# Cross parts of a recurrence in FP32 instead of split fp32r, and a layer norm written once per tile

## The reference

```python
# layer 0: Fourier mixing, then an MLP
xn = layernorm(x) ; xf = rfft2(xn)                    # per image and channel
o1 = relu(einsum(xf, w1c) + b1c)                      # blocks of 24 channels, real and imaginary apart
xs = irfft2(o1)
x  = xs + x + gelu(layernorm(xs) @ w1 + b1) @ w2 + b2 # 192 -> 768 -> 192
# layer 1: gated recurrence, then an MLP
xn = layernorm(x)
u = xn @ Wu + bu ; g = sigmoid(xn @ Wg + bg)
h = 0
for _ in range(8): h = g * (h @ A) + (1 - g) * u      # A is 192 x 192
x = x + h
x = x + gelu_tanh(layernorm(x) @ w1 + b1) @ w2 + b2
```

## Time and profile before

| | us |
|---|---|
| median of 3 runs (lowest, highest) | 1198.21 (1192.73, 1200.53) |
| the profiled execution, its own time | 1196.19 |
| span of the profile, first to last instruction | 1194.4 |
| PE matmul, PE weight load, DVE, ACT, POOL busy | 1079.7, 875.7, 853.9, 696.7, 363.5 |
| mean granted clock of the PE | 0.956 |

### The profile page before, as it was taken

The page is one execution under the profiler, slowest core; times in us unless marked ns, Lnnn a source line. Parts: engine busy times, 40 slices in busy tenths (PEclk is TensorE's granted clock), DMA queues, the critical chain, the costliest instruction groups (busy, mean ns, idle before and its releaser), DMA issues. The chain is left out here.

```text
span 1194.4 us, 26159 instructions
## 1 busy us (share of the span) xinstructions
PE 1079.7 (90%) x9256; PEld 875.7 (73%) x9256; DVE 853.9 (71%) x2230; ACT 696.7 (58%) x1293; POOL 363.5 (30%) x383
## 2 busy tenths in 40 slices
PE   3659999985797999999799999999999699999998
PEld 1358888873486888888567767767677488888887
DVE  6645556442899988777768689689698767676665
ACT  3736556542664567666677567567545266766665
POOL 1250111211699200000238438338247311021110
PEclk9879999896898999999899999999999799999999
DMA  7888799896100000000100000000000000000001
GB/s 179 272 183 169 149 168 185 154 208 163 49 1 1 0 0 0 0 0 0 47 1 2 1 1 1 1 1 1 1 1 1 0 14 27 26 27 26 26 26 40
DMA packets 140186, 64.19 MB, mean 54 GB/s; under 512 B 115808, under 2 KB 134912, under 8 KB 140096
## 3 DMA queue, kind: packets, MB, share of 16 engines
q1 hardware_dynamic: 132888, 37.42, 15.5%
q0 software_dynamic: 5568, 18.73, 5.8%
q10 hardware_dynamic: 1648, 6.91, 1.8%
HBM read 44.17 MB, written 12.58 MB: 48 GB/s over the span
## 5 line engine op out<-in xcount | busy, mean ns | idle before, releaser
L904 ACT ACTIVATE L_conv_hf<-L_conv_ps,L_conv_b 128x512 f32<-128x512 f32 x192 | 132.1, 688 | 184.4 <-PE L_conv_ps L1075 175.7
L1094 PE MATMUL L_conv_ps<-w2hl,L_conv_hhi 128*128 128x384 f32 x768 | 229.2, 366 | 4.1 <-DVE X L990 4.1
L980 DVE TENSOR_TENSOR L_conv_hlo<-L_conv_hf,L_conv_hhi 128x512 fp32r<-128x512 f32 x192 | 140.9, 750 | 78.5 <-ACT L_conv_hhi L913 76.4
L1094 PE MATMUL L_conv_ps<-w2hl,L_conv_hlo 128*128 128x192 f32 x768 | 188.6, 252 | 0.0
L1209 POOL TENSOR_TENSOR sc_lo<-XS,sc_hi 128x512 fp32r<-128x512 f32 x96 | 142.9, 1504 | 116.1 <-ACT sc_hi L1285 116.1
L1487 PE MATMUL sc_ps<-sc_hi,wh 128*128 128x512 f32 (+1 forms) x440 | 160.8, 437 | 3.4 <-ACT XS L1269 3.2
L1094 PEld LDWEIGHTS L_conv_ps<-w2hl,L_conv_hhi 128*128 128x128 f32 x768 | 144.4, 188 | 8.7 <-DVE L_conv_hlo L980 3.4
L1487 PE MATMUL sc_ps<-sc_hi,wl 128*128 128x512 f32 (+1 forms) x440 | 147.8, 392 | 0.0
L1094 PEld LDWEIGHTS L_conv_ps<-w2hl,L_conv_hlo 128*128 128x128 f32 x768 | 146.2, 191 | 0.0
L636 PE MATMUL psF<-spectrum,X 100*24 100x64 f32 x4352 | 128.9, 290 | 15.2 <-issue 11.2
L861 POOL TENSOR_TENSOR X<-X,L_conv_b 128x192 f32 x128 | 83.2, 681 | 194.4 <-DVE L_conv_xn L964 194.4
(11 more groups left out here) (135 smaller groups left out, 2028.0 us busy)
## 6 DMA issues: line engine op xcount, KB each, us to landing
X<-in_L_conv_w SPq DMA_DIRECT2D x136, 144.0 KB
XS<-in_x POOLq DMA_DIRECT2D x8, 768.0 KB, 6.9
rows_spectrum<-XS POOLq DMA_DIRECT2D x8, 768.0 KB, 4.2
d<-rows_spectrum ACTq DMA_DIRECT2D x8, 768.0 KB, 5.5
X<-in_x SPq DMA_DIRECT2D x8, 768.0 KB, 8.2
out<-X SPq DMA_DIRECT2D x15, 384.0 KB, 2.6
XS<-d POOLq DMA_DIRECT2D x59, 96.0 KB, 4.7
spectrum<-in_L_conv_mlp_w SPq DMA_DIRECT2D x2, 576.0 KB, 9.3
```

The source lines that it names most:

```text
L904: nc.scalar.activation(hf[:, m % 3, :], ps[:, RB + m % 2, :], gelu, bias=b1[:, m:m + 1]).then_inc(act1, 1)
L980: nc.vector.tensor_tensor(hlo[:, m, :], hf[:, m % 3, :], hhi[:, m, :].bitcast(F32), ALU.subtract).then_inc(h_lo, 1)
L1094: mm = pe.matmul(o, x, w, start=(m == 0 and n == 0), stop=(m == MT - 1 and n == 1), skip_group_check=True)
```

## The change

In the scan, the cross parts A01 and A10 of the state products of steps 2 to 7 (those whose state is positive and whole in one buffer) are made by one FP32 matmul each from the unsplit state, in a new function `state_product`; step 1 and the projections keep `product`. The two A01 matmuls have 64 output columns and write partitions 0 to 63 and 64 to 127 of one bank; the two A10 matmuls have 64 rows and write two banks. They stand between the high and the low parts. `mm` is counted per tile, at the three low matmuls that end the product, and ACT and POOL wait for the count of their own tile. Three more DMAs load A01 once and A10 into both halves of the partitions.

In the MLP the DVE writes each normalised tile once (192 channels), the transposes of the last channels have 64 stationary columns and alternate with the full ones, ACT writes the 64 rows of the last channels twice into `y`, and the POOL waits for the normalised tiles in the first MLP as well.

```diff
+        self.a01, self.a10 = sb("a01", [P, C1]), sb("a10", [P, P])
...
+        loads += [(self.a10[C1 * k:C1 * (k + 1), :], t["L1_conv_A"][P:C, 0:P]) for k in range(2)]
...
-        xn = sb("xn", [P, GT, 2 * P])
+        xn = sb("xn", [P, GT, C])
...
             def group(i):
-                if XS is None:
-
-                    pool.wait_ge(normed, GT * (i + 1))
+                pool.wait_ge(normed, GT * (i + 1))
...
-                    nc.scalar.activation(y[:, k, :], ps[:, TB + k, :], ACT.Identity, bias=bet[:, k:k + 1],
-                                         scale=gam[:, k:k + 1]).then_inc(y_done, 1)
+                    rows = P if k == 0 else C1
+                    for to in range(0, P, rows):
+                        ins = nc.scalar.activation(y[to:to + rows, k, :], ps[0:rows, TB + k, :], ACT.Identity,
+                                                   bias=bet[0:rows, k:k + 1], scale=gam[0:rows, k:k + 1])
+                    ins.then_inc(y_done, 1)
...
-                    for to, fr in ((slice(0, C), slice(0, C)), (slice(C, 2 * P), slice(P, C))):
-                        ins = nc.vector.tensor_scalar(xn[:, k, to], SRC[:, n, fr], mv[:, n, 0:1],
-                                                      rs[:, bass.ds(n, 1)], ALU.subtract, ALU.mult)
-                    ins.then_inc(normed, 1)
+                    nc.vector.tensor_scalar(xn[:, k, :], SRC[:, n, :], mv[:, n, 0:1], rs[:, bass.ds(n, 1)],
+                                            ALU.subtract, ALU.mult).then_inc(normed, 1)
...
-                for k in range(2):
-
-                    passed(pe, y_done, 2 * (i - 1) + k + 1)
-                    for j in range(GT):
...
+                passed(pe, y_done, 2 * i)
+                for j in range(GT):
+                    pe.wait_ge(normed, GT * i + j + 1)
+                    for k, (rows, cut) in enumerate(((P, slice(0, P)), (C1, slice(P, C)))):
+                        mm = pe.transpose(ps[0:rows, TB + k, P * j:P * j + P], xn[:, j, cut], ident[:, :])
+                        if j == GT - 1:
+                            mm.then_inc(tposed, 1)
...
-                    pool.wait_ge(q["mm"], MM * i + 3 * (s + 2))
+                    pool.wait_ge(q["mm"], MM * i + 3 * (s + 1) + (3 if s == 1 else place[j]))
...
-                            act.wait_ge(q["mm"], MM * i + 3 * (s + 2))
+                            act.wait_ge(q["mm"], MM * i + 3 * (s + 1) + (3 if s == 1 else place[j]))
...
+            def state_product(c, h, l, whole, high_in, low_in, midway=None):
...
+                bank = [ps[:, 3 * c + j, :] for j in range(3)]
+                cols = [W00["A"], W00["A"], A11]
+                for j in TILES:
+                    high_in(j)
+                    for ww in (wh, wl):
+                        pe.matmul(bank[j], ww[:, cols[j]], h[:, j, :], start=(ww is wh), stop=False, skip_group_check=True)
+                if midway:
+                    midway()
+                for j in range(2):
+                    pe.matmul(bank[2][C1 * j:C1 * (j + 1)], sh.a01[:, :], whole[:, j, :],
+                              start=False, stop=False, skip_group_check=True)
+                for j in range(2):
+                    rows = slice(C1 * j, C1 * (j + 1))
+                    pe.matmul(bank[j], sh.a10[rows, :], whole[rows, 2, :], start=False, stop=False, skip_group_check=True)
+                for j in TILES:
+                    low_in(j)
+                    pe.matmul(bank[j], wh[:, cols[j]], l[:, j, :], start=False, stop=True,
+                              skip_group_check=True).then_inc(Q[c]["mm"], 1)
...
+                if s == 1:
+                    product(c, "A", hi[c], lo[c], high_in, low_in, midway)
+                else:
+                    state_product(c, hi[c], lo[c], value(c, s - 1), high_in, low_in, midway)
```

More of the change, by code:

```diff
@@ L159, in load_vectors @@
         t, n = self.t, 0
-        loads = [(self.ident[:, :], t["ident"]), (self.inv_w[:, :], t["inv_w"])]
+        loads = [(self.ident[:, :], t["ident"]), (self.inv_w[:, :], t["inv_w"]),
+                 (self.a01[:, :], t["L1_conv_A"][0:P, P:C])]
+        loads += [(self.a10[C1 * k:C1 * (k + 1), :], t["L1_conv_A"][P:C, 0:P]) for k in range(2)]
         for name, tile_ in self.columns.items():
@@ L1564, in low_in, with high_in @@
                         pe.wait_ge(q["h_lo"], lows(i, s - 1, j))
-                product(c, "A", hi[c], lo[c], lambda j: pe.wait_ge(q["h_hi"], HL * i + 3 * (s - 1) + place[j]),
-                        low_in,
-                        (lambda: last_back(0)) if last else None)
+                def high_in(j):
+                    pe.wait_ge(q["h_hi"], HL * i + 3 * (s - 1) + place[j])
+                midway = (lambda: last_back(0)) if last else None
+                if s == 1:
+                    product(c, "A", hi[c], lo[c], high_in, low_in, midway)
+                else:
+                    state_product(c, hi[c], lo[c], value(c, s - 1), high_in, low_in, midway)
             def last_back(c):
```

## The result

| | us |
|---|---|
| before, median of 20 runs (lowest, highest) | 1197.12 (1190.28, 1202.28) |
| after, median of 20 runs (lowest, highest) | 1187.32 (1182.10, 1194.73) |
| ratio, 95% interval | 0.9927 [0.9911, 0.9943] |
| span of the profile, before and after | 1194.4, 1186.1 |

The medians lie 9.8 us apart, and the ratio puts the gain at 0.7%, clear of noise. The forecast was 1177 (range 1168 to 1222), 20 us under the median before: the sign and the scan were right, but the largest term, the POOL's wait, brought less than half of what was forecast.

The account below looks back on a forecast made before the run. It took the scan and second MLP as PE-bound, the first MLP's five early groups as bound by a DVE that the POOL slows. 1196.19 - 18.2 - 1.9 + 0.2 = 1176.3, adjusted to 1177; range 1168 to 1222.

Parts of the forecast that it names:

- the POOL's wait: First MLP: holding the POOL behind the normalised tiles makes all five early groups PE-bound, 92.48 to 74.3 us, -18.2 us.
- Scan, work per product: PE work of one state product in scan steps 2 to 7: 4.52 to 4.37 us, -0.15 us each.
- Rival B: Scan: the FP32 pairs of 512 columns don't run abreast; total 1211, or 1253 if one after another; chance 0.09.
- Scan in all: Whole scan: most of the PE's gain is lost on the DVE; -2.7 + 0.8 = -1.9 us.
- The first three pairs: Scan, pairs 0 to 2 of chains: each gains 0.9 us.
- The last pair: Scan, pair 3: 0.6 us gained before its tail, 1.4 lost in the tail, +0.8 us.
- The waits before the (4, 1) product: Scan: the (4, 1) product still waits for `hi`; 0.3 us lost up to it in pair 3.
- Rival D: Scan: gives its full 7 us, the DVE being less late than counted; total 1171; chance 0.10.
- Turns: MLP: a group's eight transposes, four now with 64 stationary columns, still take 0.87 us; cost 0.
- Rival A: MLP: turns with 64 stationary columns change the array's mode, +43.5 us, total 1220; chance 0.20.
- Normalise once, doubled by ACT: MLP: four fewer DVE instructions and one more of ACT per group change 0; +0.1 us for each of two heads.
- Rival C: First MLP: the POOL's 4.1 us always fall on `hlo` and outputs; half of 18 gained, total 1186 to 1190; chance 0.11.

Follow-up runs that it names:

- e7: Kernel before, with the DVE's second instruction of scan steps 1 and 3 shortened from 512 columns to 32; 1193.87 us, ratio 0.9994.
- e8: Changed kernel, with the DVE's second instruction of scan steps 1 and 3 shortened from 512 columns to 32; 1184.95 us, ratio 0.9911.
- e10: Kernel before, with only the POOL's group in the first MLP also waiting for the previous group's last low part; 1181.99 us, ratio 0.9866.
- e4: Changed kernel, with the POOL's group in the first MLP also waiting for the previous group's last low part; 1178.51 us, ratio 0.9851.
- e2: Kernel before, with only the POOL's wait for the normalised tiles added in the first MLP; 1196.69 us, ratio 0.9996.
- e6: On top of e4, the DVE's statistics of XS moved ahead of the group's first low part in the first MLP; 1176.00 us, ratio 0.9834.
- e12: Changed kernel, with only the POOL's long X + XS addition moved behind the group's last low part, bias additions left in place; 1179.12 us, ratio 0.9855.
- e1: Changed kernel, with the POOL's wait for the normalised tiles taken away in the first MLP; 1195.41 us, ratio 0.9988.

## Why the prediction was right and wrong

**Scan, work per product: right.** Forecast 4.37 us, measured 4.33 (two starts of the loop, 646.49 and 650.82, and steps 5 and 6 all alike).

```profile
646.49 0.39 PE L1488 MATMUL sc_ps<-sc_hi,wh 128*128 128x512 f32 x1
...
647.95 1.08 PE L1492 MATMUL sc_ps<-XS,a 128*64 128x512 f32 x4
648.96 1.13 PE L1496 MATMUL sc_ps<-XS,a 64*128 64x512 f32 x4
...
650.82 0.39 PE L1488 MATMUL sc_ps<-sc_hi,wh 128*128 128x512 f32 x1
```

The pairs run abreast: the four records of a pair span 1.08 us, where four of the 0.43 us of the forecast, one after another, make 1.7. Rival B is out. A pair with the change of mode is 1.01 or 1.06 us; I had 0.88 + 0.19. (One sum in this part was wrong, without effect on the forecast: with free changes the terms make 2.04 + 1.76 = 3.80, not 4.1.)

**Scan in all: right in kind, and luck in the number, since terms that were off cancel.** Forecast -1.9, measured -1.9. The first three pairs: -0.9, -1.2, -1.2 (the first is 557.60 to 675.31 before, 551.38 to 668.15 after), forecast -0.9 each. The last pair +1.4, forecast +0.8. Two windows for each, up to the first of the last transposes back and from there to the second MLP, first before, then after:

```profile
846.19:928.43 82.24, 81.09 (x393) 57.88 (x392) 68.52 (x133) 44.23 (x69) 43.00 (x29) 1.00 0.00 1
928.43:945.74 17.31, 7.41 (x37) 5.24 (x35) 14.52 (x30) 1.41 (x2) 4.06 (x2) 0.82 0.00 0
```
```profile
836.70:918.08 81.38, 78.77 (x344) 44.66 (x342) 68.09 (x133) 44.10 (x69) 42.13 (x29) 1.00 0.00 1
918.08:937.64 19.56, 8.93 (x36) 4.75 (x36) 14.85 (x30) 1.19 (x2) 4.63 (x2) 0.75 0.00 1
```

The body gained 0.9 (forecast 0.6), the tail lost 2.25 (forecast 1.4). From the ten transposes back to the DVE's last step I had 5.41 us (933.09 to 938.5), and it is 5.87: the pairs start 2.32 us behind the transposes' start, where the low parts started 2.05 behind it in the earlier trace rows and I took 1.7, while pairs and low parts take 3.55 us to the DVE's step, a little under my 3.7. The rest is that the ten transposes themselves come 0.6 us later behind the DVE (5.24 us from the first transpose back instead of 4.66). Over that stretch the granted clock was 0.76 instead of 0.96, behind one more wait of the PE (0.68 us) than before the change; what that alone costs no run shows. The waits before the (4, 1) product came as forecast; the one inside the (2, 1) product (703.68 instead of 703.18, ACT's `hi`) I had missed. Rival D (the full 7 us) fell for the reason given, the DVE's lateness, and e7 and e8 show it.

**Turns: right.** Rival A, to which I had given 0.20, is out. In the chain of waits a group of the second MLP is as long as it was, 1011.55 - 996.71 = 14.84 us against 14.85, and its eight transposes, four of them shown with 128*64, still take 0.87:

```profile
996.71 0.87 PE L_conv_ps L1058 x8
...
1011.55 0.87 PE L_conv_ps L1058 x8
```

**Normalise once, doubled by ACT: right, 0,** shown by e10 beside e4 (groups of 15.16 and 15.19 us) and by the second MLP's 0.2 us. Its first group, with the head, takes 14.70 us instead of 14.66, where I had +0.1. It has a side effect on the POOL's place that I didn't have (e2).

**The POOL's wait: wrong, the step that failed.** Forecast -18.2, measured -7.4. The prediction put it so: 0.36 us of DVE per us of POOL, so "the DVE's group is then 13.7 us, under the PE's 14.85", so "all five early groups become PE-bound", and of the rest only that groups "without the second set of statistics have more room"; the ten later groups got no term in the sum. Three things were wrong in it.

- The POOL's work was taken as a share of DVE time. In fact one DVE instruction is held until the POOL's one has ended (1.70 us instead of 0.68, in e2 1.72), and it counts if the PE waits for that instruction (the low part) and not otherwise (the low channels in e4, 2.22 us at no cost). The DVE was busy 13.35 of 16.07 us, no more than the 13.7 forecast, and that was no protection.
- The balance was struck over the five groups where the POOL had run. The ten that had been free of it get 4.1 us each, and paid 7.8 us: 8 of the 10.8 us missing. The other 3.0 are in the early groups themselves (-15.2 instead of -18.2): three of them have a low part held to 1.69 to 2.29 us, and two take 16.30 and 16.10 us instead of 14.9.
- A busy share under that of the bound engine says nothing where a loop of waits passes all engines: low channels (DVE), first product (PE), GELU and high part (ACT), low parts (DVE), second product (PE). Such a loop is as long as its latencies, however idle each engine is. The loop is read from the kernel's semaphores and not from a chain in a trace; the late groups of e4 and the middle groups of e6 bear it out, in which the DVE is busier than in the kernel after and the group is shorter.

Rival C named the right place ("its 4.1 us now always fall on `hlo` and the outputs") and the right time, 1186 to 1190, and I gave it 0.11, though its evidence was in the earlier trace rows: the mean of `hlo` was 1203 ns there against 686. It wasn't right throughout: the outputs aren't held (0.34 to 0.36 us each), and it halved the gain of the early groups, while most of the missing gain was lost in the ten others. (The chances didn't add up either: A and B, both slower, have 0.29 together, the summary 0.24.) The size I had forecast was there to be had: e6 has a first MLP of 223.26 us, and 241.37 - 18.2 is 223.2, but it takes the POOL's slot and the place of the statistics, not the wait alone.

The Trainium skill has the rule (SBUF — State Buffer, section "Summary: rules for kernel authors"): where a DVE instruction with two SBUF inputs meets a GpSimd one that reads SBUF, the second to issue blocks fully until the first is done, and one should "Schedule whichever is off the critical path". The traces agree for the instructions with two inputs: 1.70 us for 0.68 beside a long one; and the statistics, with one input, keep their length (e4). But instructions with one input are not all free: the copy of 128x8 is held in e4 (0.80 us for 0.17), and the 128x192 normalisations were slowed in the earlier trace rows; no run here shows what sets these apart from the statistics. I had priced a hold of single instructions as a mean rate.

## What to carry to other kernels

When one engine slows another, don't price it as a share of busy time: lay the two timelines over each other, find which single instruction will be held and for how long, and ask who waits for that one. Moving work out of a stretch that is badly bound puts it somewhere: count the groups that get it as well as those that lose it. And an engine that waits (2.69 us at the scan's end, 1.6 us in each middle MLP group) is a place to put work that is ready, without adding or removing any.

## What the runs showed that I had not expected

- A DVE instruction with two SBUF inputs that starts during the POOL's long one ends 0.54 to 0.55 us behind its end, which is most of its own 0.68: 410.71 against 410.17 after the change, 527.83 against 527.28 in e2, 494.17 against 493.62 in e4. The hold goes the other way too: the POOL's long one takes 1.84 or 1.85 us where no such instruction is running as it starts (486.40 after the change, e2, e12), and 2.11 or 2.08 where one is (408.06 after the change, 491.54 in e4).
- Two edits that each gave nothing (e1 0.9988, e2 0.9996) gave 7.4 us in the first MLP together (alone 1.5 and 0.7, inside the scatter), since one moves the instruction that the other has put in the way.
- FP32 transposes with 64 stationary columns, shown as 128*64 and alternating with full ones, cost what full ones cost (0.87 us for eight). Between matmuls of 512 columns in the scan, the step from a full one to the first with 64 columns costs 0.1 us (0.32 instead of 0.23 between starts).
